# Softplus, the router's chain and GpSimd's reads changed in a selective-scan and expert layer on one core

## The reference

```
uo = xn @ W_in.T;  u, o = halves of 256
u  = silu(conv4(u) + conv_b)
g  = u @ W_gate.T                     # 64 columns for delta, 16 for b, 16 for c
delta = softplus(g[:64] @ W_delta.T + delta_bias)
h  = exp(A * delta) * h + (delta * u) * b     # 16 states per channel, step by step
y  = (sum over states of h * c + D * u) * silu(o)
x  = x + y @ W_out.T
scores = softmax(xn2 @ gate_w.T)      # 8 experts; the two best, normalized, times 2.5
x  = x + sum of the two experts' SwiGLU (width 176) + shared SwiGLU (width 352)
```

## Time and profile before

| | us |
|---|---|
| median of three runs | 1155.44 |
| time of the profiled execution | 1155.91 |
| span of the profiled execution, first to last instruction | 1154.1 |
| one step in the steady part | 33.1 |

### The profile page before, as it was taken

One profiled execution on the slowest core, in us unless ns is written; L12 is line 12 of the kernel. 1 busy time (PEld: TensorE's weight loads), 2 busy tenths in 40 slices (PEclk: granted clock), 3 DMA queues, 4 the chain that ended last, 5 costly groups with the idle time before them and its releaser, 6 DMA issues.

```text
span 1154.1 us, 25028 instructions
## 1 busy us (share of the span) xinstructions
PE 1069.2 (93%) x8947; PEld 906.1 (79%) x8947; DVE 1051.9 (91%) x1510; ACT 1070.0 (93%) x2177; POOL 1047.6 (91%) x374
## 2 busy tenths in 40 slices
PE   4658999999999999999999999999999999998897
PEld 4436788888888888888888888888888888886786
DVE  4467999999999999999999999999999999999953
ACT  5779999999999999999999999999999999999852
POOL 3699899999999999999999999999999999999810
PEclk9567999999999999999999999999999999999999
DMA  7444444433444443334444433344444333443000
GB/s 187 110 104 112 98 121 109 105 90 89 114 116 103 121 102 106 90 94 111 120 104 121 102 100 86 103 112 110 113 121 102 92 89 104 112 99 96 6 6 10
DMA packets 71478, 115.01 MB, mean 100 GB/s; under 512 B 8173, under 2 KB 30394, under 8 KB 71354
## 3 DMA queue, kind: packets, MB, share of 16 engines
q1 hardware_dynamic: 71354, 113.42, 38.3%
HBM read 41.04 MB, written 5.24 MB: 40 GB/s over the span
## 4 chain that ended last, share of the span: by engine, by line
ACT 53%; PE 28%; issue 12%; DVE 4%; SPq 1%; DMA 1%; POOL 1%; ACTq 0%; DVEq 0%; POOLq 0%
ACT decay_ps L529 20%; PE work_ps L1023 8%; ACT g_silu L516 7%; PE work_ps L1106 6%; PE work_ps L1115 4%; PE acc_ps L1067 4%; ACT L644 3%; ACT L636 3%; ACT L678 3%; ACT L629 3%; PE acc_ps L1143 3%; ACT L697 3%; DVE features L771 2%; ACT xn L550 2%; ACT work_ps L608 2%
## 5 line engine op out<-in xcount | busy, mean ns | idle before, releaser
L437 POOL TENSOR_TENSOR inject<-rep,bc 128x2048 f32<-128x2048 f32 x128 | 581.4, 4566 | 6.2 <-DMA rep<-dd 6.2
L451 POOL TENSOR_TENSOR read<-state,bc 128x1024 f32<-128x1024 f32 x192 | 457.8, 2394 | 25.6 <-DVE state L749 22.0
L749 DVE TENSOR_TENSOR_SCAN state<-decay_ps,inject 128x1024 f32<-128x1024 f32 x192 | 438.2, 2283 | 13.5 <-ACT decay_ps L529 13.5
L529 ACT ACTIVATE decay_ps<-rep,neg_a 128x255 f32<-128x255 f32 x1024 | 426.5, 465 | 3.9 <-DVE decay_ps L764 2.2
L1143 PE MATMUL acc_ps<-ffn_down,features 128*128 128x128 f32 (+1 forms) x1792 | 235.8, 275 | 2.0 <-DVE features L779 2.0
L1143 PEld LDWEIGHTS acc_ps<-ffn_down,features 128*128 128x128 f32 (+1 forms) x1792 | 220.8, 191 | 4.9 <-DVE features L779 2.6
L1115 PE MATMUL work_ps<-xn2T_part,ffn_up 128*128 128x256 f32 x1344 | 203.6, 291 | 10.9 <-ACT g_silu L516 9.6
L1106 PEld LDWEIGHTS work_ps<-xn2T_part,ffn_gate 128*128 128x128 f32 x1344 | 171.4, 190 | 45.4 <-issue 24.7
L1106 PE MATMUL work_ps<-xn2T_part,ffn_gate 128*128 128x256 f32 x1344 | 199.8, 293 | 5.5 <-DVE features L771 5.5
L1115 PEld LDWEIGHTS work_ps<-xn2T_part,ffn_up 128*128 128x128 f32 x1344 | 173.0, 190 | 34.8 <-ACT g_silu L516 24.1
L771 DVE TENSOR_TENSOR features<-g_silu,work_ps 128x512 f32<-128x512 f32 x224 | 152.6, 681 | 25.1 <-PE work_ps L1115 22.7
(11 more groups left out here) (136 smaller groups left out, 1244.3 us busy)
## 6 DMA issues: line engine op xcount, KB each, us to landing
rep<-dd SPq DMA_DIRECT2D x256, 256.0 KB, 4.8
bc<-bc_rows SPq DMA_DIRECT2D x64, 512.0 KB, 3.9
x_in<-in_L_attn_x_dram SPq DMA_DIRECT2D x32, 128.0 KB, 2.2
out_dram<-result SPq DMA_DIRECT2D x32, 128.0 KB, 1.9
bc_rows<-g_sb SPq DMA_DIRECT2D x32, 32.0 KB
state<-in_L_ffn_w_gate_dram SPq DMA_DIRECT2D x1, 704.0 KB, 4.4
inject<-in_L_ffn_w_up_dram SPq DMA_DIRECT2D x1, 704.0 KB, 5.9
ffn_down<-in_L_ffn_w_down_dram SPq DMA_DIRECT2D x1, 704.0 KB, 7.4
```

The source lines that it names most:

```text
L437: pool.tensor_tensor(inject[:, slot:slot + many], du_all, b_all, ALU.mult).then_inc(inject_done, many)
L451: pool.tensor_tensor(read[:, slot:slot + many], state[:, first:first + many], c_all, ALU.mult).then_inc(read_done, many)
L529: last = act.activation(decay_ps[:, at % 2, j, 1:T], rep[(HALVES * n + half) % RP][:, j, 0, 1:T], ACT.Exp, scale=neg_a[:, col:col + 1])
L749: dve.tensor_tensor_scan(to, decays, inject[:, at % RI].rearrange("p j t -> p (j t)"), 0.0, ALU.mult, ALU.add).then_inc(state_done, 1)
```

## The change

- `softplus` reads `z_ps` and writes `dd` in SBUF at once. `copy_z`, `copy_delta`, `z_sb` and `delta_ps` are gone. `times_u` reads that half of `dd` in place of `delta_ps`. All three steps, softplus, `times_u` and `spread_delta`, now serve sequence k+2 at the end of step k, where they served k+1 near the step's beginning.
- The router's chain is cut in nine operations that can stand apart, with a semaphore each: `top_logit`, `shift_logits`, `best_eight`, `mark_best`, `pick_scores`, `sum_scores`, `invert_sum`, `combine`, `comb_high`, besides `comb_low`. `marked`, `inverse` and `comb` are tiles in SBUF in place of PSUM.
- `read_group` multiplies in place: the tile `read` is gone, `state` has six slots, PE sums out of `state`, and a scan waits for the sum of the sequence before in place of the read. Groups 2 and 3, and 6 and 7, are read by one instruction of 2048 elements each.
- PSUM banks of the three work banks are assigned anew, and the orders of all five engines are written anew. SP's `spread_bc` is split in two.

```
-RX, RU, RI, RS, RR, RP = 5, 3, 6, 3, 3, 3
+RX, RU, RI, RS, RR, RP = 5, 3, 6, 6, 3, 3
-GATE_BANK = [0, 1, 1, 2, 0, 2, 0]
+GATE_BANK = [1, 0, 0, 2, 2, 1, 2]
...
+        marked = sb("marked", [P, TILES, FILL + EXPERTS])
+        inverse = sb("inverse", [P, TILES])
+        comb = sb("comb", [P, TILES, EXPERTS])
...
             def read_group(n, q, many=1):
...
-                if at + many > RR:
-                    pool.wait_ge(sum_done, of_others(at + many - 1 - RR) + 1)
-                pool.tensor_tensor(read[:, slot:slot + many], state[:, first:first + many], c_all,
+                pool.tensor_tensor(state[:, first:first + many], state[:, first:first + many], c_all,
                                    ALU.mult).then_inc(read_done, many)
...
-            def copy_z(n):
-                act.wait_ge(delta_done, n)
+            def softplus(n):
                 act.wait_ge(z_mm, n + 1)
-                act.copy(z_sb[:], z_ps).then_inc(z_copied, 1)
-
-            def softplus(n):
-                act.wait_ge(z_copied, n)
-                act.activation(delta_ps, z_sb[:], ACT.Softplus).then_inc(delta_done, 1)
-
-            def copy_delta(n):
-                act.wait_ge(delta_done, n + 1)
                 for half in range(HALVES):
                     act.wait_ge(rep_in[half], 16 * JB * n)
-                act.copy(dd[:, :, 0, :], delta_ps).then_inc(dd_done, 1)
+                act.activation(dd[:, :, 0, :], z_ps, ACT.Softplus).then_inc(dd_done, 1)
...
-                dve.tensor_tensor(dd[:, :, 1, :], delta_ps, u[n % RU][:], ALU.mult).then_inc(du_done, 1)
+                dve.tensor_tensor(dd[:, :, 1, :], dd[:, :, 0, :], u[n % RU][:], ALU.mult).then_inc(du_done, 1)
...
+            def pick_scores(f):
...
-                dve.scalar_tensor_tensor(out=picked, in0=marked_ps[:, :, FILL:], scalar=1.0, in1=expd[:],
+                dve.scalar_tensor_tensor(out=picked, in0=marked[:, :, FILL:], scalar=1.0, in1=expd[:],
...
+            def invert_sum(f):
+                dve.wait_ge(denom_done, f + 1)
+                dve.reciprocal(inverse[:], denom[:]).then_inc(inverse_done, 1)
+            def combine(f):
+                dve.wait_ge(inverse_done, f + 1)
+                dve.scalar_tensor_tensor(out=comb[:], in0=picked, scalar=SCALE,
+                                         in1=inverse[:].unsqueeze(2).broadcast_to([P, TILES, EXPERTS]), op0=ALU.mult,
+                                         op1=ALU.mult).then_inc(comb_done, 1)
+            def comb_high(f):
+                dve.wait_ge(comb_done, f + 1)
                 dve.wait_ge(combT_mm, f)
-                dve.tensor_copy(comb_parts[:, :, 0:EXPERTS], comb_ps).then_inc(comb_split, 1)
+                dve.tensor_copy(comb_parts[:, :, 0:EXPERTS], comb[:]).then_inc(comb_split, 1)
...
-                dve.tensor_tensor(comb_parts[:, :, LOW:LOW + EXPERTS], comb_ps, comb_parts[:, :, 0:EXPERTS].bitcast(F32),
+                dve.tensor_tensor(comb_parts[:, :, LOW:LOW + EXPERTS], comb[:], comb_parts[:, :, 0:EXPERTS].bitcast(F32),
...
             def body(k, on, later):
                 if on(0):
                     scan(k, 0)
+                    read_own_group(k, 0)
...
```

More of the change, by code:

```diff
@@ L392, in body @@
             def body(k, on, later):
+                if later(1):
+                    spread_c(k + 1)
                 if on(-3):
@@ L631, in body @@
                     silu(k - 2, 2)
+                if later(2):
+                    norm1(k + 2)
+                if on(-2):
                     silu(k - 2, 3)
@@ L634, in body @@
                     gate_silu(k + 1)
-                if later(1):
-                    act.preload_act_table_set("softplus")
-                if on(-2):
-                    act.wait_ge(silu_done, PAIRS * (k - 2) + 4)
-                if on(-3) and not on(-2):
-                    act.wait_ge(hc_done, COMBS * (k - 3) + 6)
-                if later(1):
-                    softplus(k + 1)
-                if on(0) or later(3) or on(-1):
+                if on(0) or on(-2) or later(3) or on(-1):
                     act.preload_act_table_set("natural_log_exp_and_others")
@@ L691, in body @@
                     decays(k, 6)
+                    decays(k, 7)
                 if later(2):
-                    copy_z(k + 2)
-                if on(0):
-                    decays(k, 7)
+                    act.preload_act_table_set("softplus")
+                    softplus(k + 2)
                 if on(-1):
@@ L746, in scan @@
                 else:
-                    dve.wait_ge(read_done, count(others(n, q) - RS + 1))
+                    if n == 0 and others(n, q) == OTHERS - 2:
+                        dve.wait_ge(csel_ready, 1)
+                    if others(n, q) >= RS:
+                        dve.wait_ge(sum_done, of_others(others(n, q) - RS) + 1)
                     to = state[:, others(n, q) % RS].rearrange("p j t -> p (j t)")
@@ L916, in body @@
                     scan(k, 5)
+                    take_y(k, 0)
+                if on(-2):
+                    gated_up(k - 2, 6)
+                if on(-1):
+                    top_logit(k - 1)
+                if on(-2):
+                    weigh(k - 2, 0)
+                if on(-1):
+                    shift_logits(k - 1)
+                if on(0):
+                    scan(k, 6)
                 if on(-2):
                     weigh(k - 2, 1)
-                    weigh(k - 2, 2)
-                    weigh(k - 2, 3)
-                    weigh(k - 2, 4)
-                if on(0):
-                    scan(k, 6)
-                if on(-1):
-                    shift_logits(k - 1)
+                if later(2):
+                    times_u(k + 2)
                 if on(0):
@@ L1064, in sum_states @@
                     pe.wait_ge(read_done, others(n, q) + 1)
-                    products = read[:, others(n, q) % RR]
+                    products = state[:, others(n, q) % RS]
                 for j in range(JB):
@@ L1163, in body @@
                     ups(k - 2, 2)
+                    pe.wait_ge(silu_done, PAIRS * (k - 2) + 4)
+                if on(-3):
+                    spread_comb(k - 3, 5)
+                if on(1):
+                    pe.wait_ge(gate_done, k + 2)
+                if later(2):
+                    turn_xn(k + 2)
                 if on(-1):
```

324 lines of the change are left out of this document (148 added, 176 removed).

## The result

The changed kernel takes 1580.92 us, the median of four runs from 1578.6 to 1582.44, beside 1155.36 us for the kernel before (four runs from 1153.23 to 1155.64): a ratio of 1.3696, with a 95% interval from 1.3677 to 1.3715. The forecast was 1590. The span of the profiled execution is 1579.7 us against 1154.1.

What follows compares the result with a forecast made beforehand. ACT bound the kernel at 33.1 us a step, the other engines within 0.75; after the change 32.4 of work, 14.9 of DVE holds and 0.4 for PE added 435 us to 1154.1, giving 1590 us, range 1162 to 1650.

Steps and rivals of the forecast that it cites:

- The bound: A steady step was to be 32.4 us of work, 14.9 of holds on DVE and 0.4 for PE.
- The holds: On DVE, 13.0 us a step at `combine`, `comb_high` and `comb_low` behind scan 3, and 1.9 at `pick_scores`.
- the rest of the GpSimd instruction under way: What a held DVE operation was to wait for: nothing at least, 4.56 us at most.
- The rival in which the chain gets in first: Behind scan 3 `combine` precedes GpSimd's read; only `pick_scores` is held: 34.3 us a step, 1191 us; chance 0.14.
- The upper bound of a hold: One hold on DVE was to last 4.56 us at most, the length of one GpSimd instruction.
- The cast: `comb_high`, SBUF to SBUF on DVE, was counted as held by its pace, for 4.5 us behind a GpSimd injection.
- GpSimd's pairs: Two pairs of reads become one instruction each, 4.56 us in place of 4.75, saving 0.4 us a step.
- ACT: Dropping `copy_z` and `copy_delta` was to free 1.16 us of ACT a step, leaving about 31.6.
- PE's clock: PE, idle over 10 us ahead of `turn_comb`, gets a granted clock under 1.00, costing 0.4 us a step.
- The ends: Outside steps 2 to 29: step 30 adds 14 us, step 31 10, the start 2, the end nothing.
- The rival without holds: DVE's small operations slip between GpSimd's reads, or GpSimd alone is delayed: 32.4 to 32.6 us steps, 1136 us; chance 0.17.

## Why the prediction was right

- **The bound** moved to DVE as the prediction's sum said: 32.4 of work, 14.9 of holds and 0.4 for PE, 47.7 us a step; 47.73 were measured. The step shown above gives 32.05 of work (46.30 busy, less the holds), 14.25 of holds (4.42 + 4.42 + 1.70 + 4.40 less the operations' own 0.69) and 1.47 of idle time. Work and holds were put 1.0 us too high together, the waits 1.07 too low, and the errors cancel: that the step is right to 0.1 us is luck.
- **The holds.** For `combine`, `comb_high` and `comb_low` 13.0 us over their own time were forecast; 4.14 + 4.15 + 4.02 - 0.52 = 11.8 were measured in the mean of all 32, 12.7 in a steady step (medians 4.41, 4.42 and 4.42). The forecast's own terms, 3 x 4.56 less 0.9, give 12.8 and not 13.0. `pick_scores`: 1.9 forecast, 1.5 measured in a steady step. `times_u`: nothing forecast, and nothing measured from its fourth execution on (0.69 us, against 0.67 out of PSUM); it was nothing only because GpSimd waited for scan 7 at that moment, and where the chain went free it paid 1.5. The step on "the rest of the GpSimd instruction under way" is shown by the runs with single reads, with the chain ahead of scan 3 and with the tiles in PSUM. The rival in which the chain gets in first was close: behind scan 3, which ended at 742.39 us in the step shown, the read began 0.14 us later and `combine` 0.30.
- **The upper bound of a hold was wrong.** "4.56 us at most" doesn't hold where two GpSimd instructions follow one another: 8.5 us were seen in the kernel before with the tiles in SBUF. It didn't decide the time here.
- **The cast** was counted with the operations that need the port, from its pace in the earlier trace rows; its 4.15 us and the reduce's 0.17 in its place bear out that it is held, and leave open whether the pace was the right sign. The page "SBUF — State Buffer" of the Trainium skill, section "Who interferes with whom", names both kinds, and the trace agrees: 4.14 and 4.02 us for those with two inputs in SBUF, 4.15 for the cast, 0.17 for the reduce in its place.
- **GpSimd's pairs** took 4.565 us as wide reads (4.56 forecast), and the read's late start cost nothing by itself, as the two runs without holds show (1187.33 us with wide reads, 1185.67 with single ones). But this holds for the orders written anew alone: in the old ones GpSimd's part of the change cost 245 us, and the prediction had not looked at what stands behind the sum of group 6 on PE. The wide reads also lengthened the holds: with single reads the changed kernel was 197 us faster.
- **ACT** was busy 32.21 us in a step, 0.5 less than in the earlier trace rows and not 1.16. Its instructions overlap their neighbours when they stand close, and such overlaps count once; in the changed kernel they stand apart more often. The gain is covered in any case: ACT waits for DVE.
- **PE's clock** was 0.86 in the step shown and 0.851 over the span, as said, but the convolution took 3.10 us, as the 3.11 before, and not 5.05. What was slow stood right behind PE's 11.2 us of idle time: from 708.8 to 713.0 us the granted clock was 0.50, the lower of its levels, and `turn_comb` took 0.69 us instead of 0.44; from 716.0 on, with PE busy, it was 1.00. DVE waited 1.1 us a step for PE, in place of 0.4; how much of that is the clock wasn't separated.
- **The ends.** 28 steps gave 28 x (47.73 - 33.14) = 408.5 of the 425.6 us by which the span grew; for the start and the last steps 17 are left, where 26 were forecast.
- **The rival without holds** had its base wrong: with every hold gone the new orders, as far as the tiles in PSUM let them stand, gave steps of 34.1 to 34.5 us and 1186 to 1196 us, not 32.4 to 32.6 and 1136 (which by its own sum, 1155 less 18, is 1137). That ACT's time and the wide reads would bring 18 us without holds was not shown.

## What to carry to other kernels

- Where GpSimd multiplies all the time, keep one operand of each DVE operation in PSUM, however small the operation: 46 numbers a partition moved from SBUF to PSUM gave 284 us back. Where PSUM is full, use an operation that isn't held (a reduce for a cast), or stand right ahead of the instruction that GpSimd waits for.
- A held instruction shows as busy, not as waiting. An operation whose mean is ten times that of another of its size, and whose end falls on the end of a GpSimd instruction, was held in every case looked at here.
- Two instructions made one come back at the engine that reads them: look at what stands in its queue between the first and the second of its waits.

## What had not been expected of the hardware

- DVE can lose its turn when a GpSimd instruction ends and another follows at once: one operation on 16 numbers a partition took 8.29 us, the rest of one injection and all of the next, and this in 9 of 29 steps at that place of the kernel before with its tiles in SBUF; in the changed kernel never (59 of 59 turns won).
